# Small experts on one core: TensorE reads the ring places of two blocks with one load from a ready-made table

## What is computed

```python
logits = jnp.einsum('bsh,he->bse', hidden_states.astype(jnp.float32), router_w)
affinity = jax.nn.sigmoid(logits)
top_scores, top_idx = jax.lax.top_k(affinity, K)
top_w = top_scores / (jnp.sum(top_scores, axis=-1, keepdims=True) + 1e-09)
expert_act = jax.nn.silu(gate_out) * up_out
routed = jnp.einsum('bsei,eih->bsh', expert_act * router_mask[..., None], expert_down_k)
```

## Time and profile before

| | us |
|---|---|
| median of 3 runs | 2996.72 (2996.38 to 2997.3) |
| the profiled execution | 2986.88 |
| its span, first to last instruction | 2985.1 |
| PE busy | 2767.5 (93%) |
| DVE, ACT, POOL busy | 1517.6, 1091.5, 890.4 |
| mean granted clock of TensorE | 0.967 of full |

### The profile page before, as it was taken

One profiled execution on the slowest core, in us unless ns is written; L12 is line 12 of the kernel. 1 busy time (PEld: TensorE's weight loads), 2 busy tenths in 40 slices (PEclk: granted clock), 3 DMA queues, 4 the chain that ended last, 5 costly groups with the idle time before them and its releaser, 6 DMA issues. The chain is left out here.

```text
span 2985.1 us, 61655 instructions
## 1 busy us (share of the span) xinstructions
PE 2767.5 (93%) x18151; PEld 1904.4 (64%) x18152; DVE 1517.6 (51%) x4453; ACT 1091.5 (37%) x2869; POOL 890.4 (30%) x1692
## 2 busy tenths in 40 slices
PE   7999999999999999999789997999999999999698
PEld 5766666666666676667545554565666566656597
DVE  4445554444554444555455554565556555654432
ACT  1433333333333333333245552343334333433332
POOL 1012211212221211220244442644444444441243
PEclk9999999999999999999889998999999999999899
DMA  6000000000000000000357763100110010000251
GB/s 220 9 7 8 8 8 8 3 5 8 8 8 8 3 5 8 8 8 4 125 172 221 221 173 115 39 21 21 32 30 21 21 32 30 21 21 7 83 172 28
DMA packets 87764, 145.65 MB, mean 49 GB/s; under 512 B 22402, under 2 KB 64383, under 8 KB 86160
## 3 DMA queue, kind: packets, MB, share of 16 engines
q1 hardware_dynamic: 44304, 84.85, 9.1%
q0 software_dynamic: 20848, 41.09, 5.1%
q10 hardware_dynamic: 22544, 18.89, 1.9%
HBM read 116.17 MB, written 29.51 MB: 49 GB/s over the span
## 5 line engine op out<-in xcount | busy, mean ns | idle before, releaser
L976 PE MATMUL psG<-W,ctxT 128*125 128x512 f32 (+2 forms) x896 | 408.6, 599 | 5.2 <-DVE v L2610 5.2
L970 PE MATMUL psG<-ctxT,W 128*128 128x375 f32 (+1 forms) x1024 | 388.0, 527 | 8.1 <-issue 7.1
L970 PEld LDWEIGHTS psG<-ctxT,W 128*128 128x128 f32 x1024 | 189.9, 190 | 168.2 <-issue 115.5
L964 PEld LDWEIGHTS psG<-hT,W 128*128 128x128 f32 x2304 | 277.9, 200 | 18.4 <-ACT hT L1632 16.1
L1601 ACT ACTIVATE probs<-psG,nmax 112x375 f32<-112x375 f32 (+1 forms) x384 | 233.2, 619 | 146.1 <-DVE nmax L2015 146.0
L964 PE MATMUL psG<-hT,W 128*128 128x112 f32 x2304 | 281.7, 283 | 3.2 <-ACT hT L1632 3.2
L931 PE MATMUL psO<-probsT,v 125*64 125x112 f32 (+2 forms) x3584 | 219.7, 273 | 67.3 <-ACT probsT L1607 49.8
L976 PEld LDWEIGHTS psG<-W,ctxT 128*125 128x125 f32 (+2 forms) x896 | 159.5, 186 | 179.0 <-issue 170.9
L931 PEld LDWEIGHTS psO<-probsT,v 125*64 125x64 f32 (+2 forms) x3584 | 184.2, 143 | 139.2 <-issue 76.6
L2015 DVE TENSOR_REDUCE nmax<-psG 112x1 f32<-112x375 f32 (+1 forms) x384 | 208.6, 599 | 47.3 <-PE psG L907 47.3
L907 PE MATMUL psG<-kT,qT 64*112 64x375 f32 (+1 forms) x768 | 178.4, 545 | 9.2 <-ACT v L1858 7.4
(11 more groups left out here) (391 smaller groups left out, 4775.4 us busy)
## 6 DMA issues: line engine op xcount, KB each, us to landing
W<-in_ew SPq DMA_DIRECT2D x64, 384.0 KB
expert_rows<-W ACTq DMA_DIRECT2D x144, 128.0 KB
W<-in_ew SPq DMA_DIRECT2D x8, 2048.0 KB
ctxT<-in_ctxT SPq DMA_DIRECT2D x16, 375.0 KB, 3.2
kT<-in_ctx SPq DMA_DIRECT2D x16, 375.0 KB
normed_rows<-hrow SPq DMA_DIRECT2D x32, 112.0 KB, 1.9
W<-normed_rows,ids POOLq DMA_INDIRECT x144
slot_table<-stt,st POOLq DMA_INDIRECT x136, 4.8
```

What stands on the lines that cost most here:

```text
L964: mm = nc.tensor.matmul(bank[:, j * T:(j + 1) * T], wt[:, c, n0 + j * P:n0 + (j + 1) * P], hT[:, c, :], start=(c == 0), stop=(c == DC - 1))
L970: mm = nc.tensor.matmul(bank[:, 0:n], wt[:, c, n0 + j * P:n0 + (j + 1) * P], src[:, c, 0:n], start=(c == 0), stop=(c == DC - 1))
L976: mm = nc.tensor.matmul(bank[0:kn, 0:512], src[:, c, k0:k0 + kn], wt[:, c, n0 + half * 512:n0 + (half + 1) * 512], start=(c == 0), stop=(c ...
```

## The change

A new one-row table `urow` holds, for each block, the ring place of its upper expert, ready to use: DVE makes it with two small operations after the routing tables. PE's `load_upper` becomes one load of two registers from it, placed behind the transposes of L1336, once for each pair of blocks. The three register operations behind each load, the register `first` and PE's wait for `loaded` go.

```diff
+        urow = sb("urow", [1, L0E.NBLK], I32)
...
-                first = [pe.alloc_register(f"upper_rank{i}") for i in range(4)]
...
                 def load_upper(j, i):
 
-                    pe.reg_load(loaded_rank, brow[0:1, bass.ds(2 * j, 1)])
-                    pe.reg_alu(first[i % 4], loaded_rank, 0, ALU.max)
-                    pe.reg_alu(slots[i % UNROLL], first[i % 4], l.R - 1, ALU.bitwise_and)
-                    pe.reg_alu(slots[i % UNROLL], slots[i % UNROLL], l.wsize, ALU.mult)
+                    pe.reg_load((slots[i % UNROLL], slots[(i + 1) % UNROLL]), urow[0:1, bass.ds(j, 2)])
...
                             mm.then_inc(s.xT_full, 1)
+                        load_upper(At(turn, i, UNROLL).j, i)
                     if lo >= 2:
...
                             pe.wait_ge(s.xT_done, j.j + 1)
-                            pe.wait_ge(s.loaded, pe.snap(first[k % 4], min_val=0, max_val=l.E - 1) + 1)
                             pe.wait_ge(s.up_copied, j.j + 1)
...
                             mm.then_inc(s.gu_full, 1)
-                            if hi < 1:
-                                load_upper(At(turn, k + 2, UNROLL).j, k + 2)
-                    elif hi < 1:
-                        for k in range(i, i + 2):
-                            load_upper(At(turn, k, UNROLL).j, k)
...
                 nc.vector.tensor_scalar(lrow[:], lrow[:], 1, None, ALU.arith_shift_right).then_inc(s.tables, 1)
+                chain(nc.vector.tensor_scalar(urow[:], brow[0:1, 0:L0E.NP:2], L0E.R - 1, None, ALU.bitwise_and))
+                nc.vector.tensor_scalar(urow[:], urow[:], float(L0E.wsize), None, ALU.mult)
```

## The result

The changed kernel takes **2972.13 us** (median of 4 executions, 2970.25 to 2975.7) where the kernel before, measured with it, takes 2997.01 (2996.38 to 3005.09): a ratio of **0.9913, interval 0.9899 to 0.9927**, or 24.9 us less. The forecast was 27.7 less, 2969.0 with a range of 2957 to 2983. The profiled execution of the changed kernel took 2972.39 us, its span 2970.6, its granted clock 0.965.

A forecast was written before the change was run, and what follows sets the result against it. PE's sequencer, not its array, bounds the kernel: 0.40 us x 67 pairs = 26.8, plus some 1 for 5 other pairs, gives -27.7, so 2996.7 - 27.7 = 2969.0 us, range 2957 to 2983 (8 in 10).

The forecast's parts named there:

- The sequencer holds PE, not the array: Sequencer steps of `load_upper` between the up blocks and before the down matmuls drain the array; 0.60 us a pair by PE alone.
- Rival 3: No change: sequencer steps hidden under queued matmuls, gaps caused otherwise; 2996.7 within 6 us; chance 0.07.
- the fastest pair: Pair at 1524.65 to 1528.20 us, 3.55 us against the ordinary 4.13; PE not held since the sequencer had more lead.
- The period, 3.75 forecast: Expert stage: a pair of blocks falls from 4.15 to 3.75 us, 0.40 x 67 = 26.8 us gained.
- (a): Second silu fixed 3.63 us after the transposes; chain through DVE's product 4.63, less 0.10 for L1348, allows 3.73 a pair.
- rival 2: PE's array is the bound, the silu signal moves with PE: 3.55 to 3.6 a pair, 2956; chance 0.14.
- (b): ACT's own round, from one silu to the same one of the next pair, takes 3.70 us and limits the period.
- (c): DVE's copies of the hidden rows, behind the late product, delay the down matmuls: 0.1 to 0.2 us lost in such pairs.
- The load behind the transposes at 0: The moved load hides while the sequencer waits for DVE's product: 0; if not, once a turn, 2 to 4 us.
- rival 4: Slower: without sequencer lead, the load ahead of the hidden transposes costs 0.5 us a pair, 3033; chance 0.05.
- The clock and the transfers: In the stage the clock stays 1.00; DMA share rises from 0.73 to about 0.81, not a bound by itself.
- Outside the 67 pairs: The 5 pairs of the stage outside the counted window, of which the ramp waits for gathers: some 1 us gained.

The follow-up runs named there:

- e1: The kernel before with only PE's wait for `loaded` taken out, second chip: 2835.99 us, ratio 0.9972.
- e2: e1 plus the table, with one one-register load per block at the old places: 2824.05 us, 0.9933 (second chip); 2827.68 us, 0.9936 (third).
- e4: The changed kernel with POOL gathering only four blocks, all 144 blocks computed from those, first chip: 2959.14 us, one execution.
- e7: The changed kernel with POOL's second gather of each pair held back until that pair's up matmuls are done, third chip: 2862.9 us, 1.0058.
- e3: The changed kernel with its one two-register load behind the up matmuls instead of behind the transposes, second chip: 2825.03 us, 0.9931.

## Why the prediction was right, point by point

**The sequencer holds PE, not the array: right, and shown.** Both gaps closed where the load and its register operations went, and on the second chip e1 and e2 closed them one at a time. Over the pairs of the stage, the mean distance from the start of the last up matmul of the first block to that of the first of the second fell from 0.41 to 0.20 us, and from the up to the down matmuls from 0.48 to 0.24, where 0.20 to 0.21 is what PE takes when it waits for nothing. Rival 3, no change, falls. The Trainium skill (Advanced Engine Details and Errata, Sequencer Loop) states that other engine instructions can be read and queued while a control instruction runs; no run here contradicts that, but it doesn't follow that a load costs the array nothing, and here its steps cost array time: between 1520 and 1800 us the weight loads of before stood for issue for 38.5 us ahead of the up matmuls and 38.6 ahead of the down ones, those of the changed kernel (1527.4 to 1780.7) for 11.2 and 9.0. What had taken the sequencer's lead is shown in part only; that the fastest pair ran on a full queue, as I wrote, no row shows.

In the kernel before on the first chip the sequencer leaves the wait for the product within 0.2 us of the product's end in 34 of the 67 pairs; on the third chip in 4, and the gaps stand there all the same (24.9 and 27.7 us). So the gaps don't need a late product; the sequencer's own steps are enough.

**The period, 3.75 forecast, 3.78 measured.** The 67 pairs gave 24.6 us and not 26.8. The two gaps gave 0.45 a pair; 0.14 came back, since the first up matmul now starts 0.99 us after the pair's transposes, not 0.86; the rest is closer spacing within the blocks.

**(a), the silu at a fixed time: right, and it is what holds now on the first chip.** 3.76 on average, 3.63 forecast; e4 shows that it goes with the gathers. It doesn't move with PE's matmuls, as rival 2 had it: the last up matmul starts 0.10 us earlier in the pair than before (2.56, not 2.66), the silu 0.06 later (3.76, not 3.70).

But my number for its period came out near by luck, for two terms of the sum were off, in opposite ways. First, the size: the chain from a pair's transposes to the next pair's L1349 is 4.69 us in the pair shown (1610.89 to 1615.58), not 4.53. The silu takes 0.10 more, and of the 0.10 promised for L1348 0.06 did not come. Second, the arithmetic: I took 4.53 - 0.80 = 3.73 as the period at which the chain costs nothing, and then used it as the period that it allows. A loop through two pairs settles elsewhere. From L1349 to the next pair's transposes PE takes 2.75 (1611.82 to 1614.57), so two successive periods are 4.69 + 2.75 = 7.44, that is 3.72 each, with L1349 standing 0.97 after the transposes, as measured (0.99); the three later pairs of a turn average 3.73. With my own 4.53 the same loop gives (4.53 + 2.75) / 2 = 3.64, a gain of 0.51 x 67 + 1 = 35.2 and a time of 2961.5. The two errors, 0.08 and 0.09 a pair, cancelled. Had I done the arithmetic right, (b) at 3.70 would still have kept the forecast at 3.70 or above, and (b) was wrong in itself. So the size of the gain rests on a right mechanism and on two numbers that were right by luck.

**(b), ACT's round of 3.70: wrong.** It was 3.70 because ACT waited for the late signal, not for its own work; e4 runs it in 3.55. I had read a loop's period in a pair in which the loop was driven from outside.

**(c), DVE's copies: about right.** The gap ahead of the down matmuls is 0.03 above PE's shortest, per pair; I had 0.1 to 0.2 in some pairs.

**The load behind the transposes at 0: about right in three pairs of a turn, not in the first.** The prediction named this case, a load that doesn't fit once a turn, at the loop's branch, at 2 to 4 us, and put it at 0. On the second chip it is 3.4 us (3.83 against 3.63, where e2 has no such difference); in e4 the first pair of each turn takes 0.25 longer, and in the changed kernel on the first chip 0.2 longer (3.93 against 3.73). Elsewhere on the first chip PE waits for the late product anyway. On the second chip the first up matmul stands 0.92 after the transposes on average, against 0.83 in e2, and e7 shows what the load can cost where the sequencer has no lead (up to 1.0 us of one wait). That is the mechanism of rival 4, with its condition, lead of the sequencer, where I had put it. And the load of two registers costs 0.54 us, near the far end (0.60) of the bounds that I gave.

**The clock and the transfers: no cost, as forecast.** What DVE's two new operations cost is too small to tell. The granted clock of the stage is 1.00 before and after; the DMA share rose to 0.80 in the windows, 0.81 forecast.

**Outside the 67 pairs** I had 1 us of gain. The stage shows 0.7 of loss (23.9 against 24.6), by its tail. The other 1.0 up to 24.9 lies outside it and is within what executions differ by.

## What to carry to other kernels

Read the gap ahead of a matmul together with the sequencer's own rows: where a register load and its arithmetic stand between two matmul groups and the sequencer has no lead, its steps of 0.1 us are array time. A value that the sequencer computes each time (a masked, scaled index) belongs in a table, and a wait that another engine has already made needs no second one; that is where this gain was, not in loading two registers at once, which costs 0.23 us more than loading one. Look at the first pair behind a loop's branch by itself, for there the lead is smallest. And once a gap closes, ask which loop closes next and solve it over two rounds: its period is the mean of the two legs, not the leg less the free time.

## What the runs showed of the hardware that I had not expected

**What waits for PE's results goes on late while POOL issues indirect transfers, on one chip of three.** On the first chip the second silu starts 3.70 to 3.81 us after the transposes on average with gathers (five profiles) and 3.11 without; on the second chip, with the same gathers, at 3.18:
```profile
1501.19 0.66 PE L1333 MATMUL psG<-ident,W 128*128 128x128 f32 x4
...
1501.99 1.95 PE L1349 MATMUL psG<-W 128*64 x16
...
1503.16 0.95 POOL L712 DMA_INDIRECT W<-normed_rows,ids  x1 [0.30 <-issue]
...
1504.17 0.28 ACT L1752 ACTIVATE mlp<-psG 128x128 f32<-128x128 f32 x1
```
Silu 0.23 us behind the last up matmul's end (1503.94), where the first chip had 0.85 (1613.77 to 1614.62). These are single pairs. The batch loop of the changed kernel, on the first chip, shows what may be the same thing, larger: POOL issues a burst of scatters (L636), and DVE and ACT, idle for a signal that the profile puts down to no engine of this core, stand still for 6.2 and 7.5 us.
```profile
353.81 1.01 POOL L636 DMA_INDIRECT slot_table<-stt,st  x1 [0.79 <-POOL stt L633]
...
362.45 0.51 DVE L2019 COPY probsT<-psT 125x336 f32<-125x336 f32 x1 [6.22 <-remote]
364.56 0.45 ACT L1599 ACTIVATE probsT<-psT 125x336 f32<-125x336 f32 x1 [7.47 <-remote]
```
That it is a signal of PE is read from what the two wait for (they copy what PE wrote into psT); the profile doesn't name it, and no run takes the scatters away. The two other chips have no such waits, and the whole program takes about 150 us less there (2844 against 2997). How much of these 150 us is the same thing is not worked out: the mean granted clock is lower on the first chip too (0.964 to 0.967 against 0.984), which costs time by itself. Why the chips differ stays open. Its use for this change is plain: the gain is 24.9 us where a pair of before took 4.15, and 16.0 us (2844.03 to 2828.06) on the second chip, where by its like, the third, it took 3.93.

**Register loads.** A load of one register takes 0.30 us on PE and DVE, of two 0.53 to 0.54; on ACT 0.28 and 0.51. Two registers in one load save hardly anything over two loads (0.54 against 0.60). These are medians; in e3, where the load of two registers stands behind the up matmuls, its median is 0.81.
